# Engine orders at four places of a four-layer Flamingo kernel

## The reference

```python
x = x + tanh(g_xattn[0]) * L0_xattn(layernorm(x), ctx, wq, wk, wv, wo)        # 32 heads, 8 kv heads, D=128
x = x + tanh(g_ffn[0])   * L0_ffn(layernorm(x), W_q, scale, zero)             # 4-bit weights, 512 x 512
x = x + tanh(g_xattn[1]) * L1_xattn(layernorm(x), ctx, wq, wk, wv, wo, ln_w)  # rmsnorm * ln_w, 32 heads of 16
x = x + tanh(g_ffn[1])   * L1_ffn(layernorm(x), base_W, gate_W, A, B)         # top 2 of 28 LoRA experts
x = x + tanh(g_xattn[2]) * L2_xattn(layernorm(x), ctx, Wq, bq, Wk, bk)        # one head of 512
x = x + tanh(g_ffn[2])   * L2_ffn(layernorm(x), w1, w2, w3)                   # NF4 quantised, 1376 wide
x = x + tanh(g_xattn[3]) * L3_xattn(layernorm(x), ctx, mask, q, k, v, o, qn, kn)  # rmsnorm on q and k
x = x + tanh(g_ffn[3])   * L3_ffn(layernorm(x), ...)                          # 4 streams, 50 Sinkhorn steps
```

## Time and profile before

| | |
|---|---|
| median of 3 runs | 1448.71 us (1448.66 to 1449.44) |
| the profiled execution | 1445.92 us, its span 1444.2 us |
| TensorE busy (matmul) | 1295.6 us, 90% |
| VectorE busy | 1136.4 us, 79% |
| ScalarE busy | 760.8 us, 53% |
| GpSimd busy | 421.9 us, 29% |
| granted TensorE clock, mean | 0.964 of full speed |

### The profile page before, as it was taken

One profiled execution on the slowest core, in us unless ns is written; L12 is line 12 of the kernel. 1 busy time (PEld: TensorE's weight loads), 2 busy tenths in 40 slices (PEclk: granted clock), 3 DMA queues, 4 the chain that ended last, 5 costly groups with the idle time before them and its releaser, 6 DMA issues.

```text
span 1444.2 us, 19162 instructions
## 1 busy us (share of the span) xinstructions
PE 1295.6 (90%) x6524; PEld 988.0 (68%) x6524; DVE 1136.4 (79%) x2103; ACT 760.8 (53%) x1612; POOL 421.9 (29%) x472
## 2 busy tenths in 40 slices
PE   8999999999998989978999998999999999998105
PEld 6666566566567768746888877888888888887102
DVE  4788988898888786986555578787787777788998
ACT  4787877777743753442222235565655656555004
POOL 1112212121235560243111032523424323332720
PEclk9999999999999999999999999999999999999557
DMA  6678977897940011243211220201202202000001
GB/s 227 163 164 197 248 210 165 210 237 185 193 143 26 2 59 36 53 97 83 74 44 44 100 73 1 74 4 70 73 1 74 73 1 74 1 1 1 0 0 59
DMA packets 37914, 127.78 MB, mean 88 GB/s; under 512 B 4944, under 2 KB 10960, under 8 KB 31680
## 3 DMA queue, kind: packets, MB, share of 16 engines
q1 hardware_dynamic: 26304, 83.38, 16.9%
q0 software_dynamic: 11520, 43.26, 15.7%
HBM read 72.63 MB, written 10.75 MB: 58 GB/s over the span
## 4 chain that ended last, share of the span: by engine, by line
PE 53%; DVE 25%; ACT 7%; DVEq 6%; issue 4%; DMA 3%; POOL 1%; POOLq 1%; SPq 0%
PE PS L150 12%; PE PS L152 11%; PE PS L151 11%; DVE AR L680 5%; PE PS L1021 4%; DMA AR<-AR 2%; ACT s_sb L610 2%; DVE AR L2847 2%; DVE AR L2836 2%; DVE AR L2843 2%; DVEq L670 2%; DVE AR L686 2%; PE PS L1007 1%; PE PS L539 1%; PE PS L514 1%
## 5 line engine op out<-in xcount | busy, mean ns | idle before, releaser
L442 POOL DMA_DIRECT2D AR<-AR x76 | 75.4, 1120 | 327.5 <-DMA AR<-AR 147.5
L1316 DVE TENSOR_TENSOR R16r<-PS,R16r 64x512 fp32r<-64x512 f32 x128 | 88.1, 689 | 44.3 <-ACT R16r L1155 42.8
L151 PE MATMUL PS<-R16r 128*128 128x512 f32 (+1 forms) x328 | 122.0, 372 | 0.0
L514 PE MATMUL PS<-R,HT 128*128 128x256 f32 x512 | 116.5, 381 | 3.4 <-ACT R L599 3.4
L539 PE MATMUL PS<-R,PT 128*128 128x512 f32 x256 | 116.1, 596 | 3.5 <-DVE X L720 3.5
L152 PE MATMUL PS<-R16r 128*128 128x512 f32 (+1 forms) x312 | 119.0, 381 | 0.0
L514 PEld LDWEIGHTS PS<-R,HT 128*128 128x128 f32 x512 | 94.8, 190 | 16.4 <-ACT R L599 4.8
L610 ACT ACTIVATE s_sb<-PS,sm 128x64 f32<-128x64 f32 x256 | 78.2, 338 | 52.2 <-DVE sm L705 51.6
L1160 ACT COPY AR<-PS 128x512 f32<-128x512 f32 x64 | 37.6, 587 | 121.9 <-PE PS L152 121.9
L150 PE MATMUL PS<-HTr,R16r 128*128 128x512 f32 (+1 forms) x240 | 89.7, 374 | 4.8 <-DVE R16r L190 3.3
L150 PE MATMUL PS<-R16r,HTr 128*128 128x512 f32 (+1 forms) x224 | 89.4, 399 | 0.0
(11 more groups left out here) (340 smaller groups left out, 3677.1 us busy)
## 6 DMA issues: line engine op xcount, KB each, us to landing
AR<-AR POOLq DMA_DIRECT2D x76, 528.0 KB, 6.7
OR<-in_wo SPq DMA_DIRECT2D x12, 1024.0 KB, 12.3
dequantised<-AR SPq DMA_DIRECT2D x8, 1056.0 KB, 5.5
WR<-in_w0q SPq DMA_DIRECT2D x8, 1024.0 KB, 11.3
AR<-in_w3q SPq DMA_DIRECT2D x8, 1024.0 KB, 6.5
WR<-dequantised SPq DMA_DIRECT2D x22, 256.0 KB, 2.8
AR<-in_nf SPq DMA_DIRECT2D x4, 1056.0 KB, 9.2
nf_in<-in_nf SPq DMA_DIRECT2D x4, 1056.0 KB, 9.1
```

Of the source, the lines that this page charges most:

```text
L151: nc.tensor.matmul(out, ah, bl, start=False, stop=False)
L442: nc.gpsimd.dma_start(nf_below(g)[:, part], what[:, part], accum_op=ALU.add, max_dma_last_dim=4 * N_NF // 2).then_inc(added, 16)
L514: i = nc.tensor.matmul(bank(2 + u % 2)[:, tt * 256:(tt + 1) * 256], HT0[:, c, tok], m[:, :, c * B + b, :], start=c == 0, stop=c == C - 1)
L1316: i = nc.vector.tensor_tensor(VOl[rows, h // 2, b, :], bank(7)[rows], VOh[rows, h // 2, b, :].bitcast(F32), ALU.subtract)
```

## The change

Only orders are changed, and the cut of one weight split. Nothing is computed differently.

- *First attention, turns.* ScalarE's second `far` of a turn goes behind the first two pieces in turns 0, 2 and 3; in turn 1 it stays, and all four pieces go ahead of the exponentials. On VectorE the last `up` of group 6 moves from the end of turn 27 into turn 28, behind `shift`, and `add(29)` into turn 29, ahead of the scaling of the first feed-forward's weights.
- *Second attention, entry and weight lows.* VectorE scales and splits the tiles of the third norm earlier or later, as the diff says; TensorE makes the first scores before it turns tiles 4 and 5, and half a projection of batch 2 goes from the loop into the entry, so that turn 3 has one half instead of two. The split of the feed-forward's weights is cut in three copies (1008 columns in turn 2, 1024 in turn 7, 1024 in turn 8) and six lows (two of 504 columns in turns 4 and 5, four of 512 in turns 8 to 11). ScalarE's first key copies for the third attention go ahead of the recip spreading and the copy that waits for VectorE.
- *Third attention, softmax.* The weight lows go into other places of VectorE's order, `down(LATE, 4)` and `dve_stats(2)` go behind the stage, `up(LATE, 6)` goes next to `up(LATE, 7)`, and the sums are added in another order. GpSimd scales the second block's weights after the first unit's probabilities and ahead of one `accumulate`.
- *Fourth attention, keys.* On VectorE the keys' products go ahead of `probs_low`, and `key_norm` ahead of `norm(u + 1)`.

```diff
@@ -632,11 +632,17 @@
                     far(act, g, 2 * b + 1)
-                    far(act, g, 2 * b + 2)
+                    if b == 1:
+                        far(act, g, 2 * b + 2)
                 for h in range(2):
-                    if g + 1 < NG:
+                    if g + 1 < NG and not (b == 1 and h):
                         piece(g + 1, 4 * b + 2 * h + 1)
                         piece(g + 1, 4 * b + 2 * h + 2)
+                        if b == 1:
+                            piece(g + 1, 4 * b + 3)
+                            piece(g + 1, 4 * b + 4)
+                    if g < LATE and b != 1 and h == 0:
+                        far(act, g, 2 * b + 2)
                     if u + 2 < NU0:
@@ -758,13 +764,15 @@
                     up(dve, g, 6)
-                    up(dve, g, 7)
-                    dve.drain().then_inc(A0["nf_used"], 1)
+                    if more:
+                        up(dve, g, 7)
+                        dve.drain().then_inc(A0["nf_used"], 1)
                 if more and b == 3:
...
                 b = u % B
-                add(u - 1)
+                if b != 2:
+                    add(u - 1)
                 if b:
@@ -772,8 +780,11 @@
                 if b == 0:
+                    up(dve, LATE - 1, 7)
+                    dve.drain().then_inc(A0["nf_used"], 1)
                     dve_f0_nibbles(dve)
                 elif b == 1:
+                    add(u)
                     dve_f0_scale(dve)
@@ -1379,20 +1390,22 @@
                 else:
+                    if b == 2 and g + 1 < NG:
+                        key_products(g + 1)
                     probs_low(u)
...
                 if b == 2 and g + 1 < NG:
-                    key_squares(g + 1)
+                    key_sums(g + 1)
                 for f in folds(u, 0):
...
                     square_sum(u + 2, 0)
+                if b == 2 and g + 1 < NG:
+                    key_norm(g + 1)
                 if u + 1 < NU0:
                     norm(u + 1)
-                if b == 2 and g + 1 < NG:
-                    key_norm(g + 1)
                 for f in folds(u, 1):
@@ -1517,11 +1530,11 @@
 
-        def sum_tile(dve, s, stage, kind, banks, t):
+        def sum_tile(dve, s, stage, kind, banks, t, moments=True):
             dve.wait_ge(s["mm"], t + 1)
...
                                            X[:, t, :], ALU.mult, ALU.add).then_inc(s["acc"], 1)
-            if t % 2 and t < T - 1:
+            if moments and t % 2 and t < T - 1:
                 dve_stats(dve, t // 2)
@@ -1538,22 +1551,19 @@
             norm_scaled(dve, 2, 1)
-            sum_tile(dve, F0, 0, 1, F0_BANKS, 5)
+            sum_tile(dve, F0, 0, 1, F0_BANKS, 5, moments=False)
+            norm_scaled(dve, 2, 2)
             norm_low(dve, 2, 0)
+            norm_scaled(dve, 2, 3)
             norm_low(dve, 2, 1)
             sum_tile(dve, F0, 0, 1, F0_BANKS, 6)
-            norm_scaled(dve, 2, 2)
-            norm_scaled(dve, 2, 3)
+            dve_stats(dve, PAIRS - 2)
             sum_tile(dve, F0, 0, 1, F0_BANKS, 7)
...
             norm_scaled(dve, 2, 5)
-            norm_low(dve, 2, 4)
-            norm_low(dve, 2, 5)
-            norm_scaled(dve, 2, 6)
-            norm_scaled(dve, 2, 7)
 
@@ -1610,10 +1620,15 @@
                         i.then_inc(A1["o_split"], 1)
+                if 4 <= u < 6:
+                    half = (C * NWF - 2048) // 2
+                    cols = slice(2048 + (u - 4) * half, 2048 + (u - 3) * half)
+                    pool.wait_ge(F1["w_hi"], 1)
+                    pool_low(Wh[:, cols], Wl[:, cols], WR[:, cols])
                 c = u - NU // 2
                 if 0 <= c < C:
-                    cols = slice(c * NWF, (c + 1) * NWF)
-                    pool.wait_ge(F1["w_hi"], c // 2 + 1)
+                    cols = slice(c * D, (c + 1) * D)
+                    pool.wait_ge(F1["w_hi"], c // 2 + 2)
                     i = pool_low(Wh[:, cols], Wl[:, cols], WR[:, cols])
@@ -1743,12 +1758,11 @@
             def projections(u):
-                if u < 2:
-                    project_q(2, 0, (u,))
-                elif u == 2:
-                    project_q(2, 1, (0,))
+                if u == 0:
+                    project_q(2, 0, (1,))
+                elif u < 3:
+                    project_q(2, 1, (u - 1,))
                 elif u == 3:
-                    project_q(2, 1, (1,))
                     project_q(3, 0, (0,))
@@ -1775,16 +1789,17 @@
             pe.wait_ge(A1["v_out"], 2)
+            pe.wait_ge(F0["acc"], T)
+            pe.wait_ge(lo_ready, T + 4)
+            scores(0)
+            project_q(1, 0)
             pe_norm_tile(pe, 2, 4)
-            pe.wait_ge(F0["acc"], T)
             pe_norm_tile(pe, 2, 5)
-            scores(0)
-            pe.wait_ge(lo_ready, T + 4)
-            project_q(1, 0)
+            scores(1)
+            project_q(1, 1)
             pe_norm_tile(pe, 2, 6)
             pe_norm_tile(pe, 2, 7)
-            scores(1)
-            project_q(1, 1)
+            project_q(2, 0, (0,))
             scores(2)
@@ -1866,13 +1881,14 @@
             queries(0, 1)
-            act_norm(act, 2, range(4, T))
+            queries(1, 0)
+            act_norm(act, 2, range(4, 6))
             exps(0)
-            queries(1, 0)
             act.wait_ge(A1["o_in"], 16)
...
             queries(1, 1)
+            act_norm(act, 2, range(6, T))
             exps(1)
@@ -1882,6 +1898,9 @@
                 nc.scalar.copy(PT[:], bank(4, 2)).then_inc(A1["pt_ready"], 1)
+                if u == NU - 2:
+                    act_a2_keys(act, 0)
+                    act_a2_keys(act, 1)
                 if u + 2 < NU:
@@ -1892,15 +1911,14 @@
                 nc.scalar.copy(out1(b)[0][:, at * S:(at + 1) * S], weighed(u)).then_inc(A1["ohi"], 1)
-                if u == NU - 2:
-                    act_a2_keys(act, 0)
-                    act_a2_keys(act, 1)
+                if u == 2:
+                    act.wait_ge(F1["w_in"], 16)
+                    nc.scalar.copy(Wh[:, 2048:C * NWF], WR[:, 2048:C * NWF]).then_inc(F1["w_hi"], 1)
                 if u == 7:
-                    act.wait_ge(F1["w_in"], 16)
                     act.wait_ge(A1["q_mm"], 2 * B)
-                    nc.scalar.copy(Wh[:, 0:C * NWF // 2], WR[:, 0:C * NWF // 2]).then_inc(F1["w_hi"], 1)
+                    nc.scalar.copy(Wh[:, 0:1024], WR[:, 0:1024]).then_inc(F1["w_hi"], 1)
                 if u == 8:
-                    nc.scalar.copy(Wh[:, C * NWF // 2:C * NWF], WR[:, C * NWF // 2:C * NWF]).then_inc(F1["w_hi"], 1)
+                    nc.scalar.copy(Wh[:, 1024:2048], WR[:, 1024:2048]).then_inc(F1["w_hi"], 1)
 
@@ -1943,9 +1961,13 @@
             shift(0)
+            norm_scaled(dve, 2, T - 2)
+            norm_scaled(dve, 2, T - 1)
+            norm_low(dve, 2, T - 4)
+            norm_low(dve, 2, T - 3)
+            shift(1)
             norm_low(dve, 2, T - 2)
             norm_low(dve, 2, T - 1)
-            shift(1)
             recips(0)
@@ -2010,9 +2032,9 @@
             accumulate(pool, LATE, 2)
+            pool.wait_ge(A2["probs"], 1)
+            pool_f2(pool, (1,))
             accumulate(pool, LATE, 3)
-            pool.wait_ge(A2["probs"], 2)
-            pool_f2(pool, (1,))
             pool_norm(pool, 5)
@@ -2277,10 +2299,10 @@
             scores(0)
+            pe_f2_turn(pe, 0, 0, 2)
             pe_norm_tile(pe, 4, 6)
...
             products(1)
-            pe_f2_turn(pe, 0, 0, 2)
             scores(1)
@@ -2306,8 +2328,8 @@
             exps(0)
+            act_f2_high(act, 0, 0, 2)
             turned_scores(1)
-            act_f2_high(act, 0, 0, 2)
             probs(0)
@@ -2328,29 +2350,26 @@
                         .then_inc(A2["acc"], 1)
+            dve_f2_low(dve, 0, 0, 0)
+            dve_f2_low(dve, 0, 0, 1)
             norm_scaled(dve, 4, 6)
...
             shift(0)
-            dve_f2_low(dve, 0, 0, 0)
             norm(0)
-            dve_f2_low(dve, 0, 0, 1)
+            dve_f2_low(dve, 0, 0, 2)
             shift(1)
-            sums((0, 1))
             norm(1)
-            dve_f2_low(dve, 0, 0, 2)
-            down(dve, LATE, 4)
-            sums((2, 3))
+            sums((0, 1, 2, 3))
             dve_stats(dve, 0)
             sums((4, 5))
-            dve_stats(dve, 1)
             norm_scaled(dve, 5, 0)
             norm_scaled(dve, 5, 1)
+            dve_stats(dve, 1)
             sums((6, 7))
...
             norm_low(dve, 5, 1)
-            dve_stats(dve, 2)
 
@@ -2563,12 +2582,13 @@
             norm_low(dve, 5, 3)
+            dve_stats(dve, 2)
+            dve_stats(dve, 3)
             norm_scaled(dve, 5, 4)
             norm_scaled(dve, 5, 5)
-            dve_stats(dve, 3)
             dve_f2_low(dve, 1, 1, 0)
             dve_f2_low(dve, 1, 1, 1)
-            up(dve, LATE, 6)
+            down(dve, LATE, 4)
             norm_low(dve, 5, 4)
@@ -2578,6 +2598,7 @@
             dve.drain().then_inc(F2["acc"], 1)
+            up(dve, LATE, 6)
             up(dve, LATE, 7)
```

## The result

The changed kernel takes 1436.3 us (median of 4 runs, 1435.7 to 1438.1), where the kernel before takes 1449.1 beside it. The ratio is 0.9906, with a 95% interval of 0.9893 to 0.9919: faster by 0.9%, well outside the 0.2% that a measurement can tell from no change. By the medians the saving is 12.8 us. In a second set of runs the changed kernel had 1437.3 against 1450.1, which is 12.8 again. The forecast was 15.9 us and 1432.8; 1436.3 lies in its range and in the likeliest case's own, 3.5 us from the forecast itself.

A forecast was written before the change was run, and what follows sets the result against it. Outside the first attention PE's idle time bounds; inside it, the DVE-ACT chain. 0 + 1.2 + 3.1 + 2.2 + 1.7 + 2.7 + 5.0 = 15.9 us off 1448.7 gives 1432.8; range 1426 to 1441, likeliest case 1428 to 1437.

The forecast's parts named there:

- First attention, the loop: First attention's seven groups: PE loses its waits for pieces and runs ahead, covering the moved `far`; 0, at worst 4.9 us lost.
- First attention, its end: End of first attention: moving `up(6, 7)` and one `add` removes most of PE's 1.79 us output wait; 1.2 us gained.
- cover of 0.7 us: End of first attention: second attention's keys land at 404.5, PE needs them at 405.2 or later; slack 0.7 us.
- Second attention, entry: Second attention's entry: waits for scaled tiles (2.0) and first maxima (1.8) go, ACT's copy costs 0.6; 3.1 us gained.
- the first rival: Fourth and third attention: POOL's split holds DVE's key scaling, POOL's scaling slows DVE by 1 us; 1438.8 us, chance 0.14.
- Weight lows: Second attention: smaller weight pieces bring GpSimd's sums sooner, removing most of PE's 2.3 us wait; 2.2 us gained.
- Keys: Second attention: ACT's key copies move ahead of a result of DVE, removing PE's wait; 1.7 us gained.
- Third attention: Third attention to feed-forward: 3.71 us leaves DVE's path, 0.6 and 0.4 lost, POOL's scaling no limit; 2.7 us gained.
- Fourth attention: Fourth attention: earlier key scaling removes PE's 5.2 us wait over seven groups, not held by POOL's split; 5.0 us gained.
- The clock: Third attention's tiles and feed-forward's first product: PE may keep 2.4 GHz, 4 us more gained; 1428.8 us, chance 0.07.
- ACT waiting for pieces in the chain: First attention, turns 0, 2, 3: waits for two pieces lengthen each group by 5.6 us; 1472 us, chance 0.03.
- no change at all: Whole kernel: the four places' gains are eaten by one transfer or by the first loop; chance 0.03.

The follow-up runs named there:

- experiment 3: Changed kernel with the whole third-attention edit taken back, including its feed-forward hunks; 1432.9 us, ratio 0.9878.
- experiment 4: Kernel before with the fourth attention's edit alone; 1446.7 us, ratio 0.9976.
- experiment 6: Kernel before with the first attention's edit alone, turns and end; 1447.7 us in a single run, beside 1452.1.
- experiment 7: Kernel before with the second attention's weight lows and keys alone; 1445.5 us in a single run, beside 1452.1.
- experiment 8: Kernel before with only the key scaling moved ahead of `norm(u + 1)` in the fourth attention, product unmoved; 1447.9 us in a single run, beside 1452.1.
- experiment 5: Changed kernel with GpSimd's second block of spread keys moved behind its square roots for tiles 4 to 7; 1437.8 us in a single run, beside 1452.1.
- experiment 9: The changed kernel itself measured again, unaltered; 1437.3 us, ratio 0.9909.
- experiment 1: Changed kernel with GpSimd's third pair of accumulating transfers issued behind the norm's second pair of square roots; 1434.7 us, ratio 0.9894.
- experiment 2: Changed kernel with the third pair of accumulating transfers back ahead of GpSimd's scaling of the next weights; 1435.1 us, ratio 0.9892.
- experiment 10: Changed kernel with the third pair of accumulating transfers behind the whole norm, the fourth behind the following weight scaling; 1438.2 us, ratio 0.9914.
- experiment 11: Kernel of experiment 10 with GpSimd's second block of spread keys held until DVE has scaled tiles 2 and 3; 1434.6 us, ratio 0.9894.
- experiment 12: Changed kernel with experiment 1's transfer order and experiment 11's held spread keys together; 1432.4 us, ratio 0.9873.

## Why the prediction was right, and where it was not

The forecast came out in its range, 3.2 us too high by the sum below. That is partly luck: one term has the wrong sign, and two others gained more than was forecast. The table of stages gives the edit's effect as means over executions, old order against new, and they add up to the measured time:

```
                             forecast   old order   new order   measured
first attention                1.2       407.0       404.2        2.8
second attention, entry        3.1        81.4        79.0        2.4
second, lows and keys          3.9        63.8        60.1        3.6
third attention                2.7        63.3        65.3       -2.0
fourth attention               5.0       626.8       620.9        5.9
sum                           15.9                               12.7
```

(Old and new order are, in each line, the runs that have it: in the third attention before and experiments 3, 4, 6, 7 and 8 against changed, 5 and 9; 1, 2, 10, 11 and 12 have an order of their own there. In the entry 5, 11 and 12 are left out. The first line leaves out 3, which starts its first groups 2 us late. One execution of the old order, 8, lost 1.4 us to the clock in the line of the lows and keys; without it that line is 3.3.) The line of the third attention is the least certain, with six executions between 61.8 and 64.0 against three between 63.9 and 66.5. The medians say 12.8. The pair of profiles says 9.5, since before's third attention took 61.8 us in that one execution, 1.5 less than the mean of the old order, and the changed kernel's lost 1.3 us on the way through the fourth to the clock; the rest is in the spread of the other lines.

**First attention, the loop: 0.** The period of an undisturbed group stayed, within 0.02 us, and the far mask of turn 3 did no harm. The step "PE loses its waits for pieces, which makes it run ahead" was wrong: 8.2 of 10.5 us are left. And the loop did gain. From the first maxima of the third group to those of the eighth the ten executions of the new order take 244.1 to 244.6 us, the four of the old order 245.1 to 247.6: 2.2 as a mean, of which 0.3 is lost in the second group. The rows differ in DVE's waits for transfers: for accumulated sums 2.5 us between these marks in the profile before and 0.4 after, and in two other executions of the old order 1.8 for a load. Why the new order is spared these was not tried and stays open.

**First attention, its end: 1.2.** From the first maxima of the last group to the keys' product it is 37.9 to 38.2 us in the old order; in the new one 35.9 to 36.2 where TensorE keeps its clock, and 37.5 to 37.9 in the six of ten executions where it falls to 1.2 GHz at about 401 us. So 1.9 us at full clock, 0.9 as a mean: the size of the term is right, by other means. The 1.79 us wait of the earlier trace rows fell to 0.17, the next output then waits 2.6 us for ACT, and the source is the 3.0 us that `up(6, 7)` no longer waits (experiment 6). The keys' load was issued at 396.40, not 1.5 us later, since `up` had not become later. The forecast's cover of 0.7 us was wrong at its other end too: in experiments 1, 9 and 10, at full clock, TensorE starts on the keys at 403.0 to 403.1 and not at 405.2, and their load, issued at 396.2 to 396.5, lands 6.4 to 6.6 us later, 0.1 to 0.4 us ahead of that. So a further gain at this place would meet the load.

**Second attention, entry: 3.1, measured 1.9 in the profiles, 2.4 as a mean.** The maxima's 1.8 and ACT's 0.8 came as said. The step that failed is "which takes most of the 2.0": 1.3 are left, 1.1 of them from DVE and GpSimd side by side, shown by experiments 5, 11 and 12. That is the mechanism of the first rival, at a place where I had not looked for it. The loop started 0.4 us sooner where 1.5 were forecast (1.5 sooner with the spread keys held, experiments 11 and 12), and its fourth turn was 1.4 us shorter, where the half projection was to bring 1.6. The rest of the mean is that the old order lost 1.5 us to the clock here in two of five executions.

**Weight lows: 2.2, measured 1.5 to 1.6.** DVE's wait is 2.33 us, as forecast near 2.2, and TensorE's 2.25 us became 0.35. The fourteenth scores gave 0.4 back: I priced the wait that goes and not the next one behind it. **Keys: 1.7, measured 1.8.** Right.

**Third attention: 2.7, measured -2.0.** The one term with the wrong sign. It is off by 4.7 us, more than the whole sum is (3.2). DVE's share was right (its moments were ready 2.9 us sooner). The failed sentence is that GpSimd's scaling "starts after the first unit's probabilities instead of the second's, and so is no limit". It looked at the scaling and not at the two transfers behind it, now directly ahead of the norm's drain. Experiments 1, 2 and 10 show the drain held by transfers in flight in three orders, and each time the hold moves with them. The trace of before had the sign of it: GpSimd idle for 2.55 us at 645.91 with no releaser named, behind transfers issued at 634.9 and 637.8.

The drain explains the stretch up to DVE's first product of the feed-forward. That product comes 51.6 us after the first products of the stage as a mean of the new order and 50.7 of the old, and 47.9 and 48.0 in experiments 1 and 12, which is the forecast's 2.7 us sooner, with 1.7 us of wait still in it (against the profile before, which had the same 10.2 us at 1.2 GHz up to there, 1.3 sooner). The other 1.1 of the 2.0 us lie between the first and the second product. That stretch took 12.6 to 12.7 us at full clock in all six executions of the old order and 14.2 to 14.3 in two of the new one's three, with the clock at 1.2 GHz for 3.4 us. The forecast did not look at this place; why the clock falls there in the new order alone was not tried.

**Fourth attention: 5.0, measured 5.9.** Right, with its mechanism: the scaling started at 980.57 where 985.0 was forecast for the old timeline, which is 4.5 us later at that place. It now waits 0.56 us for GpSimd's scale and starts together with GpSimd's split; it took 1.18 us there, where it took 0.89 in the split's middle, and was not held until the split's end. What it takes without the split beside it no row of these groups shows. The wait in the rows was 0.74 us a group and the gain is 0.9; which row has the other 0.16 is open, and so is why the whole time in experiment 4 shows less.

**The rivals.** GpSimd taking back what DVE gave did come true in part: at the third attention by transfers in place of scaling, at the entry by running beside DVE. Its price for the third attention, 1.0, was too small. The clock brought nothing that shows as a gain: up to the feed-forward's first product TensorE ran at 1.2 GHz for 19.9 us as a mean of the old order and for 14.8 of the new, and still the stretch is no shorter, and behind it the new order loses time to the clock as said. ACT waiting for pieces in the chain and no change at all had no part.

## What to carry to other kernels

When a step of GpSimd moves, list its transfers with it, the next drain behind them and the reader of what they bring: here a drain cost the rest of a transfer's flight, and an idle row without a named releaser had shown it beforehand. Where a wait is taken away, price the next one behind it too (experiment 5 took 1.1 us of a wait away and brought one of 1.5; experiment 10 took away the 1.7 us that experiment 1 had left and brought 3.9). And check the terms at stage marks over several executions, since a right total can hide a term with the wrong sign.
